# The first stage of a two-layer gated cross-attention kernel: mask loads on GpSimd's DMA queue, mask counting on VectorE alone, another order of weights, values and ends

## What is computed

```python
x = x + tanh(g_xattn[0]) * L0_xattn(layernorm(x), ctx, ctx, mask, wq, bq, wk, bk, wv, bv, wo, bo)
x = x + tanh(g_ffn[0])   * L0_ffn(layernorm(x), ...)          # 8 experts, top 1, and a shared one
x = x + tanh(g_xattn[1]) * L1_xattn(layernorm(x), ctx, wq, bq, wk, bk, wv, bv, wo, bo)
x = x + tanh(g_ffn[1])   * L1_ffn(layernorm(x), ...)          # 8 experts, top 2, and a shared one
# xattn: q = x Wq^T + bq, k = c Wk^T + bk, v = c Wv^T + bv; 16 heads of 16; softmax(q k^T / 4) v; Wo, bo
# in layer 0: scores = where(mask == 0, -inf, scores)
```

## Time and profile before

| what | us |
|---|---|
| median of 3 runs | 1838.68 (1837.48 to 1839.75) |
| profiled execution, its own time | 1842.48 |
| its span, first to last instruction | 1840.7 |
| TensorE busy in the span | 1497.1 |
| VectorE busy | 1178.2 |
| ScalarE busy | 850.4 |
| GpSimd busy | 161.5 |

### The profile page before, as it was taken

How to read it: one execution, slowest core, us unless ns; L and a number is a source line. 1 busy time by engine, 2 the same in 40 slices (tenths; PEclk the granted TensorE clock), 3 DMA queues, 4 the chain that set the end, 5 groups by cost and what they waited for, 6 DMA issues and landing times. The chain is left out here.

```text
span 1840.7 us, 23843 instructions
## 1 busy us (share of the span) xinstructions
PE 1497.1 (81%) x7846; PEld 875.8 (48%) x7847; DVE 1178.2 (64%) x2318; ACT 850.4 (46%) x1524; POOL 161.5 (9%) x241
## 2 busy tenths in 40 slices
PE   6655999778896999992399999999999987857870
PEld 4222333267785888882153334334333424734550
DVE  6445999464111677766299999999999926502335
ACT  2111777622111555550217777777777783311110
POOL 2220000000200000003000000000000000151116
PEclk9885999978998999996759999999999998779995
DMA  8754222020103899971722121112112000524114
GB/s 313 274 222 136 74 53 54 16 94 25 42 1 114 299 344 338 335 270 52 218 68 69 43 41 27 24 24 45 23 23 41 6 1 1 133 74 137 41 44 137
DMA packets 108714, 196.87 MB, mean 107 GB/s; under 512 B 9006, under 2 KB 80419, under 8 KB 108615
## 3 DMA queue, kind: packets, MB, share of 16 engines
q1 hardware_dynamic: 101681, 180.71, 31.1%
q0 software_dynamic: 4608, 12.59, 2.1%
q10 hardware_dynamic: 2326, 2.31, 0.4%
HBM read 144.69 MB, written 50.36 MB: 106 GB/s over the span
## 5 line engine op out<-in xcount | busy, mean ns | idle before, releaser
L1098 DVE TENSOR_REDUCE attend_piece_max<-attend_p_bank 128x1 f32<-128x400 f32 (+3 forms) x1280 | 669.1, 589 | 68.8 <-PE attend_p_bank L986 56.7
L1078 ACT ACTIVATE attend_probs<-attend_s_bank 128x512 f32<-128x512 f32 (+1 forms) x1088 | 566.1, 601 | 244.0 <-PE attend_s_bank L997 244.0
L986 PE MATMUL attend_p_bank<-attend_k_st,attend_q_st 62*128 62x400 f32 (+2 forms) x1280 | 416.2, 435 | 55.1 <-DMA attend_k_st<-ones_rows 50.5
L997 PE MATMUL attend_s_bank<-attend_q_st,attend_k_st 64*128 64x512 f32 (+1 forms) x1088 | 401.7, 447 | 37.2 <-ACT attend_probs L1078 21.6
L997 PEld LDWEIGHTS attend_s_bank<-attend_q_st,attend_k_st 64*128 64x128 f32 (+1 forms) x1088 | 171.7, 183 | 359.6 <-ACT attend_probs L1078 350.7
L1014 PE MATMUL attend_o_bank<-attend_probs,attend_v_st 128*32 128x512 f32 (+1 forms) x2176 | 291.0, 607 | 1.4 <-ACT attend_probs L1078 1.4
L986 PEld LDWEIGHTS attend_p_bank<-attend_k_st,attend_q_st 62*128 62x128 f32 x1280 | 209.0, 194 | 103.7 <-issue 52.2
L1715 DVE TENSOR_TENSOR slots_w_low<-slots_w_up,slots_w_high 128x2048 fp32r<-128x2048 f32 x46 | 105.1, 2287 | 46.6 <-ACT slots_w_high L1711 46.6
L1525 DVE TENSOR_TENSOR share_hid<-share_b_bank,share_g_act 128x512 f32<-128x512 f32 (+1 forms) x40 | 27.5, 691 | 146.5 <-PE share_b_bank L1376 96.9
L1388 PE MATMUL share_y_bank<-share_w_dn,share_hid 128*128 128x256 f32 (+1 forms) x320 | 75.9, 398 | 25.8 <-DVE share_hid L1525 22.7
L1711 ACT ACTIVATE slots_w_high<-slots_w_up 128x2048 fp32r<-128x2048 f32 x46 | 87.7, 1909 | 6.6 <-DMA slots_w_up<-in_L_ffn_W_dram 6.4
(11 more groups left out here) (251 smaller groups left out, 1781.0 us busy)
## 6 DMA issues: line engine op xcount, KB each, us to landing
slots_w_up<-in_L_ffn_W_dram SPq DMA_DIRECT2D x46, 1024.0 KB, 7.8
slots_w_dn<-in_L_ffn_W_dram SPq DMA_DIRECT2D x23, 1024.0 KB, 5.8
prep_raw<-in_mask_BxSxS_ik_dram SPq DMA_DIRECT2D x16, 800.5 KB, 10.3
attend_q_st<-q_rows SPq DMA_DIRECT2D x64, 192.0 KB, 4.6
k_rows<-prep_k_part SPq DMA_DIRECT2D x12, 800.5 KB, 6.9
attend_k_st<-k_rows SPq DMA_DIRECT2D x32, 300.2 KB, 5.7
q_rows<-prep_q_part SPq DMA_DIRECT2D x12, 512.0 KB, 8.4
sorted<-keep_zeros SPq DMA_DIRECT2D x6, 1024.0 KB, 8.8
```

Source lines behind the costliest of these rows:

```text
L986: last = pe.matmul(bank[:, 0:even(kn)], q_st[rows, slot, t * P:(t + 1) * P].bitcast(F32R), k_st[rows, slot, k0:k0 + even(kn)].bitcast(F32R ...
L997: last = pe.matmul(out, k_st[rows, hs, kt * P:kt * P + kn].bitcast(F32R), q_st[rows, hs, q0:q0 + CH].bitcast(F32R), start=True, stop=not m ...
L1078: act.activation(probs[0:kn, (kt + hs) % RING, q0:q0 + CH], s_bank[(NC * kt + c + hs) % RING][0:kn, :], ACT.Exp).then_inc(exp_done, 1)
L1098: dve.tensor_reduce(dst, bank_of(i, n)[:, 0:kn], AX.X, ALU.max).then_inc(entry_done, 1)
```

## The change

In `prepare` alone, and one list of semaphores beside it:

- The 16 mask loads leave SyncE's program and stand in GpSimd's, which first waits for all of x, and then for a free buffer before each load from the fifth on. Their semaphores are made once for the whole kernel.
- GpSimd counts nothing. There is one sum `masked`, and VectorE counts all 16 tiles: one after each low part of key units 0 and 1 (eight), one after each low part of the queries (eight), none between value tiles.
- TensorE turns four weights ahead of the keys of layer 0 instead of two. ScalarE copies four there, ahead of the square root.
- ScalarE copies the context out of the banks, VectorE does not.
- The mask sums run ahead of value tile 4, the turned ends ahead of value tile 9; VectorE finds the ends after value tile 5, and the window ahead of layer 1's low parts.
- SyncE loads weights 4 to 7 ahead of the query stores, and stores the row of hidden keys ahead of key units 2 and 3.

```diff
-            for n, t in enumerate(on_pool):
-                pool.wait_ge(landed[t % RR], 16 * (t // RR + 1))
-                pool.wait_ge(counted[1], n + 1)
-                pool.tensor_scalar(flag[:, :], raw[:, t % RR], 0.0, None, ALU.is_equal).then_inc(flagged, 1)
-                pool.wait_ge(flagged, n + 1)
-                pool.tensor_tensor(masked[1][:, :], masked[1][:, :], flag[:, :], ALU.add).then_inc(counted[1], 1)
+            for n in range(4):
+                pool.wait_ge(x_in[n], 16)
+            for t in range(QT):
+                if t >= RR:
+                    pool.wait_ge(counted, t - RR + 2)
+                pool.dma_start(raw[:, t % RR], io["mask_BxSxS2_ik0"][0, t * P:(t + 1) * P, :]).then_inc(landed[t % RR], 16)
...
-            for t in range(RR):
-                load_mask(t)
             for n in range(2, WR):
                 load_weights(n)
             store_keys(0)
-            load_mask(4)
             store_keys(1)
-            for t in range(5, 9):
-                load_mask(t)
+            for n in range(WR, NW):
+                load_weights(n)
             for n in range(4):
                 store_queries(n)
-                load_mask(9 + n)
-            for n in range(WR, NW):
-                load_weights(n)
-            for t in range(13, QT):
-                load_mask(t)
             for kt in range(KT):
                 store_values(kt)
+            sp.wait_ge(row_copied, 1)
+            sp.dma_start(scratch["key_mask"].rearrange("a (k p) -> (a k) p", p=P), hidden_row[:, :]).then_inc(row_stored, 16)
             for u in (2, 3):
                 store_keys(u)
...
-            for n in range(2):
+            for n in range(WR):
                 turn_weight(n)
...
-            for n in range(2, WR):
-                turn_weight(n)
             pe.wait_ge(w_copied, WR)
             for kt in range(KT):
+                if kt == 4:
+                    add_masks()
+                if kt == 9:
+                    turn_ends()
                 bank = take(1, b_bank, v_added, kt + 1)
...
+            for kt in range(KT):
+                kn = keys_of(kt)
+                act.wait_ge(c_turned, kt + 1)
+                act.activation(c_t[:, :, kt * P:kt * P + kn],
+                               b_of("c", kt)[:, 0:DB * P].rearrange("p (b k) -> p b k", b=DB)[:, :, 0:kn], ACT.Copy)\
+                    .then_inc(c_copied, 1)
...
                                              in1=k_part[:, u % KR, 0, k0:k0 + kn], op0=ALU.add, op1=ALU.subtract)\
                         .then_inc(k_low, 1)
+                    count_masks(masks)
...
-            split_keys(0)
+            split_keys(0, 1)
             dve.wait_ge(rooted, 1)
             dve.reciprocal(inv[:, :], std[:, :]).then_inc(inverted, 1)
-            count_masks(1)
-            split_keys(1)
+            split_keys(1, 1)
...
-                if n % 2 == 0:
-                    count_masks(1)
+                count_masks(1)
...
-                count_masks(1)
-            count_masks(len(left))
-            find_ends(dve, unseen, key, score, hidden[:, :], touched[:, :], ends, numbered, scored)
-            split_keys(2)
-            split_keys(3)
+                if kt == 5:
+                    find_ends(dve, unseen, key, score, hidden[:, :], touched[:, :], ends, numbered, scored)
             dve.wait_ge(ends_turned, 1)
             dve.tensor_copy(hidden_row[:, :], unseen[0:KT, P:2 * P]).then_inc(row_copied, 1)
             find_window(dve, turned_ends, choice, window, ends_turned, stepped)
+            split_keys(2)
+            split_keys(3)
```

More of the change, by code:

```diff
@@ L198, in prepare @@
         b_in, bv_in = sc.sem("b_in"), sc.sem("bv_in")
-        landed = [sc.sem(f"landed{n}") for n in range(RR)]
-        flagged = sc.sem("flagged")
-        one_made, counted = sc.sem("one_made"), [sc.sem("counted_dve"), sc.sem("counted_pool")]
+        landed = const["pool_landed"]
+        one_made, counted = sc.sem("one_made"), sc.sem("counted")
         c_turned, c_copied = sc.sem("c_turned"), sc.sem("c_copied")
@@ L221, in prepare @@
         per = -(-(KT - 1) // LOADS)
[L222 to L228, removed]
         @block.gpsimd
@@ L348, in keys, with add_masks, turn_ends @@
                 last.then_inc(k_ready, 1)
+            def add_masks():
+                pe.wait_ge(one_made, 1)
+                pe.wait_ge(counted, QT + 1)
+                for kt in range(KT):
+                    kn = keys_of(kt)
+                    last = pe.matmul(unseen[0:kn, kt:kt + 1], masked[:, kt * P:kt * P + kn], ones[:, :], start=True,
+                                     stop=True)
+                last.then_inc(scored, 1)
+            def turn_ends():
+                pe.wait_ge(scored, 18)
+                pe.transpose(unseen[0:KT, P:2 * P], hidden[:, :], const["ident"][:, :])
+                for n in range(2):
+                    last = pe.transpose(turned_ends[:, n], ends[:, n:n + 1], const["ident"][:, :])
+                last.then_inc(ends_turned, 1)
             for kt in range(KT):
@@ L395, in _ @@
                 turn_weight(n)
[L396 to L402, removed]
-                    last = pe.matmul(unseen[0:kn, kt:kt + 1], masked[n][:, kt * P:kt * P + kn], ones[:, :],
-                                     start=(n == 0), stop=(n == 1))
-            last.then_inc(scored, 1)
+            pe.wait_ge(w_copied, WR + 1)
             for u in (2, 3):
                 for c in range(NP):
-                    pe.wait_ge(w_copied, WR + 1)
                     keys(u, c)
-            pe.wait_ge(scored, 18)
-            pe.transpose(unseen[0:KT, P:2 * P], hidden[:, :], const["ident"][:, :])
-            for n in range(2):
-                last = pe.transpose(turned_ends[:, n], ends[:, n:n + 1], const["ident"][:, :])
-            last.then_inc(ends_turned, 1)
-        a_items = ([("w", n) for n in range(2)] + [("k", n) for n in range(DB * NP)] + [("q", n) for n in range(2 * NC)]
-                   + [("w", n) for n in range(2, NW)] + [("k", n) for n in range(DB * NP, 2 * DB * NP)])
+        a_items = ([("w", n) for n in range(WR)] + [("k", n) for n in range(DB * NP)] + [("q", n) for n in range(2 * NC)]
+                   + [("w", n) for n in range(WR, NW)] + [("k", n) for n in range(DB * NP, 2 * DB * NP)])
         b_items = [("c", n) for n in range(KT)] + [("x", n) for n in range(QT // 2)] + [("v", n) for n in range(KT)]
@@ L480, in _ @@
                                ACT.Identity, bias=q_bias[:, b:b + 1]).then_inc(q_high, 1)
-            for n in range(2, NW):
+            for n in range(WR, NW):
                 copy_weight(n)
@@ L487, in _ @@
         def _(dve):
-            left = list(on_dve)
+            left = list(range(QT))
             def count_masks(n):
@@ L2034, in flamingo_kernel @@
             "scattered": [ctx.enter_context(nc.semaphore(f"scattered{l}")) for l in range(2)],
+            "pool_landed": [ctx.enter_context(nc.semaphore(f"pool_landed{n}")) for n in range(4)],
             "gathered": [[ctx.enter_context(nc.semaphore(f"gathered{l}_{t}")) for t in range(QT)] for l in range(2)],
```

32 lines of the change are left out of this document (9 added, 23 removed).

## The result

The changed kernel took 1819.88 us (median of 6 runs, 1815.57 to 1825.96), the kernel before 1839.22 us beside it (6 runs, 1834.27 to 1843.05). The ratio is 0.9897, 95% interval 0.9874 to 0.9920: about 19 us less. The profiled execution took 1815.57 us with a span of 1813.8 us.

A forecast was written before the change was run, and what follows sets the result against it. No one engine bounded the stage: transfers and compute took turns, with stores waiting behind mask loads. Layer 1's keys at 103.0 instead of 123.3 us gave -20.3 us, from 1838.7 to 1818.4; range 1810 to 1831.

The forecast's parts named there:

- Weights ahead of K: Start of the stage: K starts at 25 us, its first low part at 27.7 instead of 26.36, +1.3 us.
- Context copies on ScalarE: Start of the stage: 13 copies, 4 to 8 us in all from 11.4 us, done by 19.5, costing nothing.
- Counts in the K phase: Layer 0's keys: eight counts between low parts wait for mask tiles; the last ends at 50.5 us, not 46.1.
- x: Normalisation loop after layer 0's keys: falls from 10.22 to about 7.0 us, ending at 57.5; first query low part 60.6.
- GpSimd's issue: Mask loads from GpSimd's queue: 1.0 us taken for each issue, hidden, with bounds of 0 to 4 us.
- Queries: Query phase: eight pieces take 19.6 us, to 80.2; the last mask tile, at half rate, makes it 81.
- Values: Value phase: tile 4 waits for tile 0's store until 87 us; values end at 100.9, layer 1's keys start at 103.0.
- Transfers alone: Rival, 15%: in this stage only the 25.8 MB of transfers decide, gaining 23 to 26 us; 1812 to 1815 us.
- Stores did not starve: Rival, 13%: mask rows beat query rows in the shared engines, delaying query stores; gain 9 to 12, 1826 to 1830 us.
- The null case: Rival, 4%: the order of the stage's mask loads did not matter and nothing is won; within 3.6 us, 1838.
- GpSimd's queue is no bound: Rival, 8%: GpSimd's queue holds up VectorE's counts; slower from 4.8 us a mask tile, 1858 us at 6 us.
- The signs that it named: Marks expected in the stage's profile after, such as value tile 4 near 87 us and layer 1's keys from 103.

The follow-up runs named there:

- the kernel with the queue alone: The kernel before with only the mask loads on GpSimd's queue and all counts on VectorE, eleven of them behind value tiles: ratio 0.9887.

## Why the prediction was right, point by point

The time came out at 1819.88 us, forecast 1818.4. The mechanism was in the main the one forecast: the stores no longer stand behind a mask load that waits, and VectorE's chain and the bytes end close together. The stage gave 18.0 us where 20.3 were counted. That it came so near is partly luck, since misses cancelled in two places (x and values, below), and the last step had the wrong wait.

**Weights ahead of K**: K starts at 23.86 us, not 25, and the first low part at 27.49 (forecast 27.7). The table load fell behind the weight copies as said.

**Context copies on ScalarE**: all done by 17.85 us (forecast 19.5), 0.3 to 0.4 us each. No cost, and no gain that a ratio shows.

**Counts in the K phase**: waits for mask tiles of 2.25, 1.49 and 1.48 us, 5.2 in all where 4 were forecast, from the sixth tile on and not the fifth. Tiles came 3.86 us apart (forecast 4.0). The last count ends at 51.4 (50.5).

**x**: each normalisation 405 to 413 ns, no more 3.367 us; the loop ends at 57.4 (57.5), the first query low part at 60.42 (60.6). It started 0.9 us late, behind the counts, and took 6.1 us where 7.0 were taken (10.22 less 2.96 is 7.3): two misses that cancel. With GpSimd's addition gone no normalisation is held, here or in the kernel with the queue alone (407 to 414 ns).

**GpSimd's issue**: 0.53 us a tile, where 1.0 was taken between bounds of 0 and 4. The first four took 0.59 us each. The rule that its descriptor writing starves behind VectorE's two-port modes (the Trainium skill, SBUF — State Buffer, "Who interferes with whom") showed nothing here: the one issue that lies inside the x loop, at 51.69 us, took 0.53 us as the others did. No row says in which mode those operations ran.

**Queries**: tiles 3.2 us apart, not 4.0: they got 61% of what the engines moved (0.82 MB in 3.2 us are 256 of 420 GB/s), beside query rows that are shorter. The half share was too low here, in the bound that was given. Still the last count ends at 82.9 and not 81: pieces without a wait took 2.39 us (2.45), but tile 12, handed over at 62.9 us as the first after the x loop, came only at 71.2, and the three behind it could not catch that up. ScalarE's wait for the query store did not go, but fell to 2.6 us. It cost nothing: VectorE was later.

**Values**: here the step was wrong. Value tile 4 was forecast at 87 us after a wait for the first value store, with tiles 4 to 6 already multiplied. TensorE had only three banks, filled with tiles 0 to 2, and stood 6.8 us until VectorE's counts were over. It then ran tile 3 at half clock, 3.78 us where 1.8 were counted. The table of TensorE's stretches around it:

```profile
78.00:83.50 5.50, 0.00 (x0) 0.00 (x0) 4.83 (x5) 0.00 (x0) 0.00 (x0) 0.87 1.02 418
83.50:87.30 3.80, 3.77 (x10) 1.52 (x11) 1.17 (x2) 0.00 (x0) 0.00 (x0) 0.50 1.02 419
87.50:97.00 9.50, 9.50 (x28) 4.30 (x25) 4.61 (x22) 0.00 (x0) 0.00 (x0) 0.93 0.56 194
```

Tile 4 was added at 90.18, and it waited for TensorE, not for the store. From 83.53 the ten tiles 3 to 12 took 20.7 us: 3.78, nine times 1.72, and 1.4 for sums, ends and edges. Forecast were six tiles and the ends, 11.4 us, from 89.5. So the values were multiplied by 104.2 us instead of 100.9, and the keys started at 105.79 instead of 103.0. In all 9.3 us more of work began 6.0 us earlier, and the miss is only 3.3 us, of which the slow tile is 2.0.

**The rivals.** Transfers alone gave the bound that the experiments found: with the counts out of the way the first value store decides (89.64), and with three tiles less in front it comes 5 to 6 us earlier. Stores did not starve: masks took 61% at most. The null case did not come. Its premise held all the same: the bytes are unchanged, and so is the rate of full stretches (about 420 GB/s in both). GpSimd's queue is no bound at 0.53 us a tile. What the prediction missed is the sign of one part. It had all 13.1 MB of masks ahead of the value store in its 25.8 MB, and never asked whether they had to be: with the counts left in their old places three tiles stay behind the store, and the stage ends 5.0 us earlier. It also took GpSimd's counts as a cost to VectorE alone, and not as what held the last mask load until 96 us.

**The signs that it named.** Held: the first low part, no normalisation over 0.5 us, 383 GB/s from 22 to 57 us and 391 from 62 to 86 on average, though single stretches fell to 373 and 291. Not held: no wait of ScalarE for the query store (2.6 us), and value tile 4 near 87 us behind a wait of VectorE for the store (90.18, behind TensorE). The waits in K came from the sixth tile on, and the keys 2.8 us late.

## What to carry to other kernels

A load that waits for a free buffer must not stand in a queue ahead of stores whose data is ready; a second issuing engine is the easy way, an order by time on one queue does nearly as well. Look also at who frees that buffer: one slow consumer among fast ones holds up the queue. When transfers run at full rate, count the bytes in front of the store that is waited for, and remember that consuming early frees buffers early and calls in more of them. Before moving work into a gap, ask whether the transfer it triggers is wanted before or after those that are on the path.

## What was not expected of the hardware

- A plain load from GpSimd's queue, 128 rows of 6.4 KB, held GpSimd 0.53 us; the indirect DMA of 128 rows took 0.99 us.
- Two queues shared nearer to row length than by halves, in the two phases seen here: beside key stores with rows of 6.4 KB the mask queue got 212 GB/s (0.82 MB in 3.86 us), half of the total, and beside query rows of 4 KB 256 GB/s (3.2 us), 61%.
- A TensorE pause of 6.8 us was followed by 3.8 us at a granted clock of 0.50, in which one value tile took 3.78 us and not 1.8; the pause that VectorE's counts cause costs more than its own length. In the kernel before a value tile also took 3.78 us behind a pause of 19.9 us.
- A VectorE count of 1.82 us took 3.63 and 4.23 us beside GpSimd's counting in the kernel before, and 1.82 or 1.83 us in all 16 places once GpSimd counted nothing.
